# The last expert's stored weights waited for in the first mixture, and the linear attention's signal to VectorE given for every two tiles

## What is computed

```python
x = x + attn_a(layernorm(x))   # linear attention, 8 heads of 8
x = x + ffn(layernorm(x))      # dense branch + mixture of 8 experts, 2 per token
x = x + attn_b(layernorm(x))   # causal softmax attention, one head of 256
x = x + ffn(layernorm(x))      # the same weights again

# attn_a:  q, k, v = x @ Wqkv;  context = einsum('bhnd,bhne->bhde', softmax(k), v)
#          out = (q @ context) @ Wout + bout
# ffn:     xn = layernorm(x) * gamma + beta
#          abel = gelu(xn @ abel_w + abel_b);  top-2 of xn @ gate_w
#          moe  = sum of w_e * (gelu(xn @ ew1[e] + eb1) @ ew2[e] + eb2), times expm(gens[0..2])
#          x + abel * (1 - gate) + moe * gate
```

## Time and profile before

| | |
|---|---|
| median of 3 runs | 1405.59 us (1405.02 to 1406.62) |
| the profiled execution | 1404.93 us, of which its span, first to last instruction, 1403.3 us |
| mean granted TensorE clock | 0.900 |
| busy: PE / PEld / DVE / ACT / POOL | 1130.2 / 985.6 / 875.0 / 497.5 / 412.9 us |
| share of the span: PE / PEld / DVE / ACT / POOL | 81% / 70% / 62% / 35% / 29% |
| moved by DMA | 161.20 MB, mean 115 GB/s |

### The profile page before, as it was taken

The page is one execution under the profiler, slowest core; times in us unless marked ns, Lnnn a source line. Parts: engine busy times, 40 slices in busy tenths (PEclk is TensorE's granted clock), DMA queues, the critical chain, the costliest instruction groups (busy, mean ns, idle before and its releaser), DMA issues. The chain is left out here.

```text
span 1403.3 us, 25721 instructions
## 1 busy us (share of the span) xinstructions
PE 1130.2 (81%) x7112; PEld 985.6 (70%) x7113; DVE 875.0 (62%) x2780; ACT 497.5 (35%) x953; POOL 412.9 (29%) x478
## 2 busy tenths in 40 slices
PE   6796996982699999953899989997960899999930
PEld 5663774872589998942789978896860789989920
DVE  6436764887366666636776667545774566666658
ACT  1011562342244444421333333332440434444435
POOL 3001110477344444420000000001676344444410
PEclk9898997697799999986899999998795999999975
DMA  9400242258543333333011100000466753433357
GB/s 286 153 0 0 99 161 101 76 202 275 177 156 91 105 91 91 91 121 118 1 46 46 46 13 35 1 1 1 166 224 220 237 193 105 135 105 102 107 177 240
DMA packets 75439, 161.20 MB, mean 115 GB/s; under 512 B 11270, under 2 KB 36562, under 8 KB 75354
## 3 DMA queue, kind: packets, MB, share of 16 engines
q1 hardware_dynamic: 54794, 104.93, 21.8%
q0 software_dynamic: 19776, 54.45, 13.0%
q10 hardware_dynamic: 784, 0.79, 0.2%
HBM read 88.66 MB, written 71.47 MB: 114 GB/s over the span
## 5 line engine op out<-in xcount | busy, mean ns | idle before, releaser
L1453 PE MATMUL bank<-ew,rows 128*128 x852 | 298.2, 350 | 4.4 <-DVE rows L1088 2.7
L1454 PE MATMUL bank<-low_in,rows 128*128 x852 | 273.1, 321 | 0.0
L1455 PE MATMUL bank<-ew,rows 128*128 x852 | 272.8, 320 | 0.0
L1240 POOL DMA_INDIRECT results<-xh x142 | 141.6, 997 | 294.2 <-DVE xh L1116 280.2
L1453 PEld LDWEIGHTS bank<-ew,rows 128*128 128x128 f32 x852 | 161.8, 190 | 15.4 <-issue 8.5
L1455 PEld LDWEIGHTS bank<-ew,rows 128*128 128x128 f32 x852 | 161.3, 189 | 12.0
L1454 PEld LDWEIGHTS bank<-low_in,rows 128*128 128x128 f32 x852 | 162.4, 191 | 6.0
L1335 ACT ACTIVATE xh<-bank 128x512 f32<-128x512 f32 x142 | 85.0, 599 | 219.1 <-PE bank L1455 219.1
L1125 DVE TENSOR_TENSOR rows<-bank,rows 128x512 fp32r<-128x512 f32 x142 | 98.2, 691 | 95.2 <-ACT rows L170 86.0
L606 POOL TENSOR_TENSOR work<-work,mhalf 128x8 f32<-128x8 f32 (+1 forms) x20 | 37.9, 1894 | 403.4 <-DVE work L599 403.3
L1221 POOL DMA_INDIRECT slots_in<-xh,work x128 | 127.3, 994 | 49.7 <-issue 36.6
(11 more groups left out here) (317 smaller groups left out, 2029.0 us busy)
## 6 DMA issues: line engine op xcount, KB each, us to landing
xh<-slots_in POOLq DMA_DIRECT2D x142, 129.0 KB, 2.7
low_in<-low SPq DMA_DIRECT2D x32, 512.0 KB
xh<-results SPq DMA_DIRECT2D x14, 1032.0 KB, 5.5
residual<-xs SPq DMA_DIRECT2D x16, 512.0 KB, 5.9
dense<-ab SPq DMA_DIRECT2D x16, 512.0 KB, 7.5
xs<-residual SPq DMA_DIRECT2D x16, 512.0 KB, 4.4
ab<-dense SPq DMA_DIRECT2D x9, 512.0 KB, 8.6
xs<-in_L_attn_a_x_dram SPq DMA_DIRECT2D x4, 1024.0 KB
```

Of the source, the lines that this page charges most:

```text
L1240: pool.indirect_dma_start(out=yg, out_offset=bass.IndirectOffsetOnAxis(ap=back[j % RING], axis=0), in_=yr[j % RING], in_offset=None).then_ ...
L1453: pe.matmul(o, hi, f32r(high(c)), start=(c == 0), stop=False)
L1454: pe.matmul(o, hi, f32r(low(c)), start=False, stop=False)
L1455: last = pe.matmul(o, lo, f32r(high(c)), start=False, stop=(stop and c == chunks[-1]))
```

## The change

Two edits. First, the four stores of the last expert (e = 7) raise `x_in` in place of `st1`, `st2` and `st_high`. SP at the end of `context()` waits for the stores of the first seven experts alone. `x_in`, which stands at 16 x 8 from the inputs' loads, ends at 16 x (8 + 4), and this is waited for in `mixture(0)` by DVE ahead of `normalise(0)`, and by SP ahead of its first store. Second, `attend` adds 1 to `att_ps` after every two tiles, and DVE waits for one count ahead of each of its two additions.

```diff
                     for n in range(2 * E):
+                        e, end = n // 2, n // 2 == E - 1
                         if n % 2 == 0:
-                            e = n // 2
                             sp.wait_ge(rest1_ok, KC * (e + 1))
-                            sp.dma_start(low1[e], rest1[e % 2].rearrange("p c h -> p (c h)")).then_inc(st1[e % 2], 16)
+                            sp.dma_start(low1[e], rest1[e % 2].rearrange("p c h -> p (c h)")).then_inc(x_in if end else st1[e % 2], 16)
                         sp.wait_ge(rest2_ok, n + 1)
-                        sp.dma_start(low2[n // 2][:, n % 2 * HH * C:(n % 2 + 1) * HH * C], rest2[n % 4].rearrange("p h c -> p (h c)")
-                                     ).then_inc(st2[n % 4], 16)
+                        sp.dma_start(low2[e][:, n % 2 * HH * C:(n % 2 + 1) * HH * C], rest2[n % 4].rearrange("p h c -> p (h c)")
+                                     ).then_inc(x_in if end else st2[n % 4], 16)
                         if n % 2:
-                            sp.dma_start(high2[n // 2].rearrange("p (h c) -> p h c", h=HC), ew2[:, :, n // 2, :]).then_inc(st_high, 16)
-                    sp.wait_ge(st_high, 16 * E)
+                            sp.dma_start(high2[e].rearrange("p (h c) -> p h c", h=HC), ew2[:, :, e, :]).then_inc(x_in if end else st_high, 16)
+                    sp.wait_ge(st_high, 16 * (E - 1))
                     for k in range(2):
-                        sp.wait_ge(st1[k], 16 * E // 2)
+                        sp.wait_ge(st1[k], 16 * len(range(k, E - 1, 2)))
                     for k in range(4):
-                        sp.wait_ge(st2[k], 16 * 2 * E // 4)
+                        sp.wait_ge(st2[k], 16 * len(range(k, 2 * (E - 1), 4)))
...
+            STORED = 16 * (8 + 4)
...
                         if r == 0:
-                            v.wait_ge(att_ps, g + 1)
                             for h in range(2):
+                                v.wait_ge(att_ps, 2 * g + h + 1)
                                 x2 = xs[:, g * GT + 2 * h:g * GT + 2 * h + 2, :].rearrange("p t c -> p (t c)")
                                 v.tensor_tensor(x2, x2, bank[:, h, :], ALU.add).then_inc(x1_ok, 1)
...
                     statistics(1)
+                    if r == 0:
+                        v.wait_ge(x_in, STORED)
                     normalise(0)
...
+                    if r == 0:
+                        sp.wait_ge(x_in, STORED)
                     assert E == NG
...
                                              start=True, stop=True)
-                        last.then_inc(att_ps, 1)
+                            if t % HALF == HALF - 1:
+                                last.then_inc(att_ps, 1)
```

## The result

Over 20 runs the changed kernel has a median of 1402.34 us (1398.73 to 1405.85); the kernel before, in 20 runs beside it, has 1405.66 us (1403.32 to 1409.52). The medians differ by 3.3 us. The ratio is 0.9975, interval 0.9967 to 0.9984: **faster by 3.5 us, between 2.2 and 4.6**, by a quarter of a per cent. The forecast was 1401.3 in a range of 1399.2 to 1404.2. The profiled execution took 1400.59 us, its span is 1399.0 us, and the granted clock is 0.899 in the mean (0.900 before).

A forecast was written before the change was run, and what follows sets the result against it. SP, waiting for the last stores, alone holds the seam's barrier some 3 us; behind it PE and DVE take turns. Roots gain 2.9 + 1.28 + 0.5 = 4.7, slots 4.76; less 0.4, 4.3: 1405.59 to 1401.3 us, range 1399.2 to 1404.2.

The forecast's parts named there:

- The wait leaves the seam: At the end of `context()`, SP reaches its drain at about 229.2 in place of 232.1, a gain of 2.9 us.
- The drain as a rival: At the seam, SP's drain itself lasts until the stores have landed, so the 2.9 us stay; 1403.9 us, chance 0.12.
- The new waits cost nothing: DVE's wait ahead of `normalise(0)` and SP's ahead of its first store are covered by ten microseconds and cost nothing.
- Two halves, 1.28 us: DVE's first addition runs during `attend(0)` and `attend(1)`, so `attend(2)`, `normalise(0)` and `turn(0)` come 2 x 0.64 us earlier.
- 0.5 us at `statistics(5)`: At g = 5, DVE's idle 0.52 us ahead of `statistics(5)` goes, about 0.5 us gained for the roots, not for PE.
- The slack of 0.58 us in the slots: The slots of g = 1 are ready 0.58 us ahead of the roots' end, so their gain is 4.76 us.
- The clock, 0.4 us: PE's clock rise at `dense(0)` stays a little behind the earlier work, a loss of 0.4 us.
- The bound of 2.1 us on the other side: At most 2.1 us gained, if PE's clock rises at the first pass of `dense(0)`.
- The sum: Over the whole kernel, the gains at roots and slots less 0.4 for the clock give 4.3 us.
- The checkpoints: Instants expected in the profile: double roots about 273.3, last scatter's end about 351.7, first expert matmul about 359.4.
- The clock did not eat the gain: Rival: clock rises at `dense(0)` and the experts both come later in the work, costing 1.5 and 1 us; 1403.4, chance 0.10.
- the rise slipping into `dense(1)`: Rival: PE's clock rise misses `dense(0)` and PE stays low until `dense(1)` ends; 1410.3 us, slower, chance 0.05.

The follow-up runs named there:

- seam_only: The changed kernel with one attend signal per group again, so the stores' wait moved alone; 1431.39 us, ratio 0.9981 against the kernel before.
- rank_early_c: The changed kernel with `rank(1)` ahead of `dense(1)` on PE, first kind of chip; 1399.59 us in nine runs, ratio 0.9954 against the kernel before.
- rank_early_b: The changed kernel with `rank(1)` ahead of `dense(1)` on PE, first kind of chip; one execution of 1396.41 us.
- best_b: The changed kernel with `rank(1)` ahead of `dense(1)` and no release between `context()` and `mixture(0)`, first kind of chip; 1398.79 us, ratio 0.9952 against before.
- best: The changed kernel with `rank(1)` ahead of `dense(1)` and no release between `context()` and `mixture(0)`, chip 15; 1436.43 us, ratio 0.9948 against before.
- before_again: The kernel before, unchanged, on chip 15 of the second kind; 1443.03 us in one execution.
- after_again: The changed kernel, unchanged, on chip 15 of the second kind; 1438.97 us in eight runs, ratio 0.9973 against the kernel before.

## Why the prediction was right, and which step failed

- **The wait leaves the seam, 2.9 us.** Right: 2.93, and seam_only shows it alone. SP comes to its branch at 229.4 and its drain is over at once.
- **The drain as a rival.** It fell. SP's drain took 17 ns at 229.6, while the stores, the last issued at 229.14, still moved until about 232. POOL's drain at the end of the mixture lasts 5.12 us again, as in the earlier trace rows. The Trainium skill (PSUM — Partial Sum Buffer, "Engine vs sequencer instructions") says that a drain waits for the engine to go fully idle. By this row a transfer that SP has handed on does not count as the engine's work.
- **The new waits cost nothing.** Right. The stretches show the stores gone soon after 232, DVE comes to `normalise(0)` at 242.6, and no wait on a DMA appears there in SP's or DVE's list.
- **Two halves, 1.28 us.** Right: 1.27, additive. The signals themselves cost nothing that a row shows: the idle time ahead of `attend(1)` and `attend(2)` fell from 1.45 and 1.38 us (seam_only) to 0.78 twice, by an addition's 0.64 within a few hundredths.
- **0.5 us at `statistics(5)`.** Right at its place (0.47), and worth nothing, since the slots bind.
- **The slack of 0.58 us in the slots: the step that failed.** I compared the end of `locate` with the end of the roots, but an index starts a transfer on POOL only 0.8 us later. Before, roots and slots were due together, and 264.12 against 263.15 in the same trace would have warned me. In place of "2.9 + 1.28, plus the slack of 0.58, 4.76" stand 4.2 less the clock's 0.44, 3.76, and 3.74 was measured at the first scatter. rank_early_c gets 0.56 of the slack back.
- **The clock, 0.4 us.** Measured 0.44 in the run of 32 (9.65 for 9.21), which begins with `route(1)` and is not `dense(0)` alone, as I had it; nothing in the sum hangs on that. The number came out, the reason only in part: the rise did not follow the work but came after a low stretch of fixed length, shorter by 3.4 us than before, and why it was shorter is not known. That 4.2 less 3.3 leaves 0.9, of which half is lost, is luck as far as my argument goes. The bound of 2.1 us on the other side was too narrow: in rank_early_b the rise came before `dense(0)`, and its run of 32 ended 35.17 us after `ctxm`, where before less 4.2 gives 38.06. That is 2.9 us more on PE than the 4.2; 1.35 reached the first scatter (46.21, rank_early_c 47.56).
- **The sum.** 4.3 was forecast, 3.5 (2.2 to 4.6) measured. The interval holds 4.3, so the time does not show a shortfall; the first scatter does, 3.74, and the missing slack accounts for it. The span of exactly 1399.0 is partly luck: at the end of the first mixture the gain is 2.3 (2.7 from the common instant), and the second mixture gives 1.9 back for no reason in the change. The checkpoints were off accordingly: roots 273.73 for 273.3, which is the 0.41 by which `context()` came later; the end of the last scatter 353.10 for 351.7 and the first expert 360.63 for 359.4, which is that and the 0.6 of the slots, and 0.2 to 0.4 more among the scatters.
- **The other rivals.** The clock did not eat the gain (0.44 of it), and no profiled execution shows the rise slipping into `dense(1)`, though in best_b it came 0.58 us before the end of the run of 32; the slowest of the 20 runs, 1405.85, is far from 1410.3.

## What to carry to other kernels

A barrier that waits for stores whose reader is far away makes every engine pay for them, here 2.9 us; moving the wait to the first reader cost nothing, with a cover of some ten microseconds. When two chains meet at one instruction, compare when the instruction could start by each, the lag in front of it included, and not when their last producers end: a slack of 0.58 us on paper was none. The lag can be read in the trace at hand, wherever the same kind of instruction waits for one producer alone. And where a clock rise lies in the path, judge an edit of a few tenths by instants in the rows, not by the time of the whole: work that came sooner under an unmoved rise kept only half of its gain on PE.

## What the hardware did that I had not expected

- **From DVE's index to an indirect transfer on POOL: 0.8 us.** 0.80 in the changed kernel, 0.78 or 0.79 in 15 more places, 0.96 or 0.97 at the first such transfer of every trace, against 0.20 to 0.21 behind POOL's own instruction when the index has been ready for longer.
- **A drain means different things.** SP's ended in 17 ns with a transfer open. POOL's at the end of the first mixture lasted 5.12 us, up to 620.6, which is 1.4 us longer than SP needed to see the last transfer land (619.2); what it waits for there is not shown.
- **PE stays at 1.2 GHz through 20 us of uninterrupted work** (246.2 to 266.8 in the changed kernel), **and one program can rise 10 us apart** (27.04 and 37.55 us after `ctxm`, rank_early_b and rank_early_c; 26.04 and 37.37, best and best_b). The low stretch around the seam had three lengths in fourteen executions: 30.7, 41.0 and 44.4 us.
- **On the second kind of chip engines pause in the routing without a releaser in the trace.** In before_again the list of waits from 230 to 375 us has (us in total, times, longest)

```profile
ACT work L170 <- remote: 21.3, 2, 15.0
DVE work L1011 <- remote: 19.6, 2, 12.2
```

and in after_again

```profile
ACT work L170 <- remote: 27.0, 4, 8.7
DVE work L1014 <- remote: 19.4, 4, 7.2
```

("remote" stands where the trace names no instruction and no transfer of this core as what ended the wait.) The first expert of after_again comes 15.6 us later than the changed kernel's on the first kind (146.88 for 131.27); the whole execution is 26 us longer (1426.57 for 1400.59), and it was the fastest of its eight, whose median is 1438.97. The cause was not tried and stays open; the gain by the change is the same fraction.
